# Last batch of a gated SSM + ternary FFN kernel worked tile by tile in halves of 512 columns, roundings on VectorE, a new order of all pieces

## The reference

```python
z = layernorm(x)
# selective state-space layer over ctx, 256 channels e, 16 states n, 256 steps l
u = silu(causal_conv4(in_proj @ ctx) + conv_b)
dt, Bm, Cm = split(x_proj @ u)                 # 8 + 16 + 16 rows
delta = softplus(dt_proj @ dt + dt_b)
state[e,n] = state[e,n] * exp(delta*A[e,n]) + delta*u*Bm[n]      # along l
y = (sum_n state*Cm[n] + D*u) * silu(z)
x = x + tanh(g_xattn) * y
# feed-forward with ternary weights and 8-bit tokens
h = layernorm(x)
q  = round(h * 128/absmax(h)) ; gate, up = q @ Wg, q @ Wu        # 256 -> 1024
i  = fwht(silu(gate) * up)                     # Walsh-Hadamard over 1024
q2 = round(i * 128/absmax(i)) ; x = x + tanh(g_ffn) * (q2 @ Wd)  # 1024 -> 256
```

## Time and profile before

| what | value |
|---|---|
| median of 3 runs | 239.27 us (238.29 to 240.78) |
| the profiled execution's own time | 238.49 us |
| its span, first to last instruction | 236.4 us |
| granted TensorE clock, mean | 0.909 |
| busy: DVE, PE, POOL, ACT | 78%, 75%, 71%, 70% |
| last store issued to the end | some 2 us |

### The profile page before, as it was taken

How to read it: one execution, slowest core, us unless ns; L and a number is a source line. 1 busy time by engine, 2 the same in 40 slices (tenths; PEclk the granted TensorE clock), 3 DMA queues, 4 the chain that set the end, 5 groups by cost and what they waited for, 6 DMA issues and landing times.

```text
span 236.4 us, 3708 instructions
## 1 busy us (share of the span) xinstructions
PE 177.0 (75%) x1216; PEld 144.1 (61%) x1216; DVE 185.4 (78%) x270; ACT 165.5 (70%) x285; POOL 168.6 (71%) x262
## 2 busy tenths in 40 slices
PE   3876859988987977788778599956746987575864
PEld 2545637977866966476677467745633776433752
DVE  3518986799999996999978946997668885579962
ACT  2499999996999983999956479968445614733230
POOL 1003079996799999999999999999999999500000
PEclk9985575599999999999979979999999999998895
DMA  3795000000000000000000000000000000000001
GB/s 65 224 348 217 1 1 0 4 0 0 3 0 3 0 0 4 0 0 1 3 1 0 0 0 3 22 25 1 0 0 3 24 22 3 0 22 0 3 22 44
DMA packets 8148, 6.33 MB, mean 27 GB/s; under 512 B 2202, under 2 KB 7874, under 8 KB 8130
## 3 DMA queue, kind: packets, MB, share of 16 engines
q1 hardware_dynamic: 7154, 6.02, 8.0%
q10 hardware_dynamic: 976, 0.09, 0.3%
HBM read 5.05 MB, written 1.05 MB: 26 GB/s over the span
## 4 chain that ended last, share of the span: by engine, by line
POOL 41%; ACT 21%; PE 15%; issue 9%; DVE 8%; DMA 3%; SPq 1%; POOLq 0%; DVEq 0%; ACTq 0%
POOL driveT L1276 11%; POOL wnat L1340 9%; POOL wnat L1341 9%; ACT decay L983 7%; POOL wq L1298 5%; DMA ctxs<-in_ctx_dram 3%; PE PY L468 2%; PE GP L598 2%; POOL q L1294 2%; DVE wnat L1604 2%; DVE wnat L1615 2%; ACT wq L1098 2%; DVE wnat L1614 1%; PE X L497 1%; PE BC L407 1%
## 5 line engine op out<-in xcount | busy, mean ns | idle before, releaser
L1276 POOL TENSOR_SCALAR driveT<-duT,BT 128x256 f32<-128x256 f32 x120 | 56.9, 500 | 13.7 <-ACT duT L1000 10.9
L983 ACT ACTIVATE decay<-delta,zero_c,aneg 128x255 f32<-128x255 f32 x128 | 64.9, 588 | 0.8 <-DVE state L1478 0.7
L1478 DVE TENSOR_TENSOR_SCAN state<-decay,BC 128x512 f32<-128x512 f32 x30 | 36.4, 1213 | 9.8 <-issue 6.9
L1478 DVE TENSOR_TENSOR_SCAN state<-decay,UP 128x512 f32<-128x512 f32 x30 | 36.1, 1203 | 5.7 <-issue 3.3
L1555 DVE TENSOR_TENSOR prod<-state,BC 128x1024 f32<-128x1024 f32 x32 | 38.3, 1198 | 1.1 <-DVE state L1478 0.8
L468 PE MATMUL PY<-id,prod 128*128 128x128 f32 x256 | 35.5, 284 | 1.4 <-DVE prod L1555 0.9
L468 PEld LDWEIGHTS PY<-id,prod 128*128 128x128 f32 x256 | 30.5, 147 | 3.0 <-DVE prod L1555 1.6
L1340 POOL TENSOR_TENSOR wnat<-wnat 128x512 f32<-128x512 f32 x18 | 22.9, 1274 | 0.9 <-DVE wnat L1604 0.2
L1341 POOL TENSOR_TENSOR wnat<-wnat 128x512 f32<-128x512 f32 x18 | 22.9, 1274 | 0.0
L1102 ACT COPY hT<-GP 128x1024 f32<-128x1024 f32 x8 | 8.1, 1008 | 21.2 <-PE GP L616 21.2
L407 PE MATMUL BC<-id,driveT 128*128 128x128 f32 x120 | 19.8, 291 | 3.2 <-POOL driveT L1276 2.2
(11 more groups left out here) (210 smaller groups left out, 390.5 us busy)
## 6 DMA issues: line engine op xcount, KB each, us to landing
wnat<-in_L_ffn_w_gate_dram SPq DMA_DIRECT2D x1, 1024.0 KB, 9.4
xs<-in_x_dram SPq DMA_DIRECT2D x1, 1024.0 KB, 11.8
wnat<-in_L_ffn_w_up_dram SPq DMA_DIRECT2D x1, 1024.0 KB, 11.9
wnat<-in_L_ffn_w_down_dram SPq DMA_DIRECT2D x1, 1024.0 KB, 11.3
out_dram<-ot SPq DMA_DIRECT2D x8, 128.0 KB, 1.7
ctxs<-in_ctx_dram SPq DMA_DIRECT2D x1, 384.0 KB, 6.9
ctxs<-in_ctx_dram SPq DMA_DIRECT2D x1, 128.0 KB, 2.7
inw<-n_L_xattn_in_proj_w_dram SPq DMA_DIRECT2D x1, 128.0 KB, 2.7
```

The lines of the kernel that those rows point to most:

```text
L983: last = nc.scalar.activation(decay[:, m % RING, h, n, 1:L], delta[:, b % 2, h, 1:L], ACT.Exp, bias=zero_c[:], scale=aneg[:, h, NB * j + n ...
L1276: last = nc.gpsimd.tensor_scalar(driveT[:, m % RING, c, n], duT[:, b % 2, c], BT[:, b % 2, c, NB * j + n:NB * j + n + 1], 1.0, ALU.mult, A ...
L1478: nc.vector.tensor_tensor_scan(state[:, g % STATES, h].rearrange("p n l -> p (n l)"), decay[:, g % RING, h].rearrange("p n l -> p (n l)"), ...
```

## The change

It has three parts.

1. **The roundings leave POOL.** `round_tokens_early` and `round_down_early` are gone. `round_tokens(f)` and `round_down(f, t)` on DVE do all of them. POOL's `second_rstd(3)` is gone too; DVE does it in `last_second_rstd`.
2. **The last batch in pieces.** Everything from the residual of batch 3 on has functions of its own, `last_...`, for one tile of 128 tokens, and from `last_gate` on for half of its 1024 columns, so one bank of PSUM. After the folds a half holds the even or the odd blocks of 128. The maximum of a tile is that of its halves, so `last_quant` waits for both. `q2_T` and `down` write into the banks that the Hadamard product used. Copies out of PSUM that DVE made for the last batches (`tokens_out`, `q2_out`) are ACT's now.
3. **A new order** of the pieces on PE, ACT, POOL and DVE from the first one on. Of these lists the diff below shows a few lines.

```diff
@@ POOL: gone @@
-            def round_tokens_early(f):
-                pool.wait_ge(act_xr, f + 1)
-                nc.gpsimd.tensor_scalar(q[:], xn[:], MAGIC + QB - 1, MAGIC, ALU.min, ALU.subtract).then_inc(rounded, 1)
-            def round_down_early(f, t):
-                pool.wait_ge(act_tq, LC * f + t + 1)
-                nc.gpsimd.tensor_scalar(q2[:, t], tq, MAGIC + QB - 1, MAGIC, ALU.min, ALU.subtract).then_inc(rounded_down, 1)
@@ ACT @@
+            def last_silu(t, i):
+                act.wait_ge(last_gated, 2 * t + i + 1)
+                act.wait_ge(last_gs, t + 1)
+                nc.scalar.activation(sg[:, t, 512 * i:512 * (i + 1)], last_half(ffn_bank(B - 1, t), i), ACT.Silu,
+                                     bias=zero_c[:], scale=gs[:, t:t + 1]).then_inc(last_sg, 1)
+            def last_quant(t, i):
+                act.wait_ge(last_sc, t + 1)
+                if t == 0:
+                    act.wait_ge(dve_q2, LC * (B - 1))
+                else:
+                    act.wait_ge(last_q2, i + 1)
+                nc.scalar.activation(tq[:, 512 * i:512 * (i + 1)], last_half(transform_bank(B - 1, t), i), ACT.Identity,
+                                     bias=magic_c[:], scale=sc2[:, t:t + 1]).then_inc(last_tq, 1)
...
@@ DVE @@
+            def last_second_rstd(c):
+                link = last_link[c]
+                dve.wait_ge(last_stat, c + 1)
+                dve.wait_ge(last_r, c + 1)
...
+            def last_absmax(t, i):
+                link = last_link[t]
+                dve.wait_ge(last_h, 2 * t + i + 1)
+                col = am3[:, t, i:i + 1]
+                link(nc.vector.tensor_reduce(col, last_half(transform_bank(B - 1, t), i), AX.X, ALU.max,
+                                             apply_absolute_value=True))
...
+            def last_round_down(t, i):
+                dve.wait_ge(last_tq, 2 * t + i + 1)
+                half = slice(512 * i, 512 * (i + 1))
+                nc.vector.tensor_scalar(q2[:, t, half], tq[:, half], MAGIC + QB - 1, MAGIC, ALU.min, ALU.subtract
+                                        ).then_inc(last_q2, 1)
@@ PE @@
+            def last_inter_T(t, i):
+                pe.wait_ge(last_folded, 4 * t + 3 + i)
+                if t == 1:
+                    pe.wait_ge(last_hT, i + 1)
+                for j in range(NI // 2):
+                    a = 2 * j + i
+                    last = nc.tensor.transpose(last_half(GP, i)[:, P * j:P * (j + 1)], fold[:, t, P * a:P * (a + 1)], id32[:])
+                last.then_inc(pe_last_tp, 1)
...
@@ order, ACT, start @@
-            for_silu()
             first_tap()
+            for_silu()
+            tanh_gates()
             xpw_out()
@@ order, POOL @@
             second_rstd(2)
-            round_down_early(1, 0)
+            drives(28)
             drives(29)
-            round_tokens_early(2)
+            drives(30)
             token_factors(2)
-            drives(30)
             drives(31)
-            round_down_early(1, 1)
```

More of the change, by code:

```diff
@@ new lines, in last_by, with last_gate @@
+            def last_by(t, i, w, done):
+                for h in range(HALF):
+                    last = nc.tensor.matmul(last_half(ffn_bank(B - 1, t), i), qT[:, h, P * t:P * (t + 1)],
+                                            w[:, h, 512 * i:512 * (i + 1)], start=(h == 0), stop=(h == HALF - 1))
+                last.then_inc(done, 1)
+            def last_gate(t, i):
+                pe.wait_ge(last_qT, t + 1)
+                if t == 0:
+                    pe.wait_ge(act_tp, LC * (B - 1))
+                else:
+                    pe.wait_ge(act_tq, LC * (B - 1) - 1)
+                last_by(t, i, wgT, last_gated)
@@ new lines, in last_hadamard @@
+            def last_hadamard(t, i):
+                pe.wait_ge(last_hT, 2 * t + i + 1)
+                if t == 0:
+                    pe.wait_ge(act_tq, LC * (B - 1))
+                else:
+                    pe.wait_ge(last_mul, 2 * LC)
+                for j in range(NI // 2):
+                    last = nc.tensor.matmul(last_half(transform_bank(B - 1, t), i)[:, P * j:P * (j + 1)],
+                                            hT[:, t, 2 * j + i, :], had[:], start=True, stop=True)
+                last.then_inc(last_h, 1)
@@ new lines, in last_q2_T, with last_down @@
+            def last_q2_T(t, i):
+                pe.wait_ge(last_q2, 2 * t + i + 1)
+                for j in range(NI // 2):
+                    last = nc.tensor.transpose(last_half(transform_bank(B - 1, t), i).bitcast(BF16)[:, P * j:P * (j + 1)],
+                                               q2[:, t, 512 * i + P * j:512 * i + P * (j + 1)], id16[:])
+                last.then_inc(pe_last_q2T, 1)
+            def last_down(t, i):
+                pe.wait_ge(last_q2T, 2 * t + i + 1)
+                for j in range(NI // 2):
+                    last = nc.tensor.matmul(transform_bank(B - 1, t)[:, 0:E], q2T[:, t, NI // 2 * i + j, :],
+                                            wdT[:, 2 * j + i, :], start=(i == j == 0), stop=(i == 1 and j == NI // 2 - 1))
+                if i == 1:
+                    last.then_inc(pe_dn, 1)
@@ L1238, in _ @@
             second_norm(2)
+            decays(30)
             for_silu()
@@ L1715, in _ @@
             times_C(6)
+            weight_out(1)
             scan(8, 0)
@@ L1780, in _ @@
             times_C(22)
-            result(0, 0)
             scan(24, 0)
@@ L1786, in _ @@
             scan(25, 0)
+            result(0, 1)
             scan(25, 1)
             times_C(24)
+            residual(2)
             scan(26, 0)
-            result(0, 1)
-            residual(2)
+            stats2(2, dve_ln_link)
+            absmax2(1, 0)
             scan(26, 1)
             times_C(25)
-            stats2(2, dve_ln_link)
-            absmax2(1, 0)
+            round_down(1, 0)
             scan(27, 0)
@@ L1798, in _ @@
             times_C(26)
-            scan(28, 0)
             token_scale(2, dve_ln_link)
             absmax2(1, 1)
+            round_tokens(2)
+            scan(28, 0)
             scan(28, 1)
+            round_down(1, 1)
             times_C(27)
+            result(1, 0)
             scan(29, 0)
```

652 lines of the change are left out of this document (381 added, 271 removed).

## The result

The changed kernel takes **224.08 us** (median of four runs, 223.40 to 224.99), against 239.17 us before (238.29 to 240.78): a ratio of 0.938, 95% interval 0.934 to 0.943. The forecast was 223.5 us. The profiled execution took 223.4 us, with a span of 221.6 us (before 236.4).

The account below looks back on a forecast made before the run. POOL was taken to bound the kernel from step 10 to the last sum in PY. Gains of 9.8 (roundings), 0 (start) and 5.3 us (last batch) took the profiled 238.49 us to 223.4, predicted as 223.5, range 218 to 231.

Parts of the forecast that it names:

- The sum of the middle: From step 10's `times_C` to the last sum in PY: DVE's 98.8 us plus 6 idle, 104.8 us, gain 9.8.
- The total: Whole kernel: gains of 9.8 + 0 + 5.3 = 15.1 us, giving 223.5 us.
- The idle time: DVE's in the middle: 2.1 us for the last sum, 2.6 walked, 1.3 for PE's queue, 6 us in all.
- The bound passes from POOL to DVE: In the middle, POOL's work falls from 112.3 to 91.9 us and DVE's rises to 98.8, so DVE binds.
- The chain's shares: In the chain of waits, POOL's share falls from 41% to under 15% and DVE's rises over 30%.
- The start: Up to step 10: one more open table load, 1.3 us, other moves offsetting; counted 0, 1.5 us either way.
- The last batch: From the last sum in PY to the last result: 32.6 us in four pieces against 37.9, gain 5.3 us.
- B: In the steps, DVE's idle time comes back as waits for ACT, 13 us idle; 230.5 us, chance 0.26.
- C: In the last batch, PE runs its small pieces at the low clock, 3 us more; 226.5 us, chance 0.09.
- D: Roundings in DVE's queue before scans wait for ACT at seven places, 19.2 us; 241.3 us, chance 0.05.
- E: POOL stays the bound because DVE locks it out, half of its 20.4 us kept; 228.5 us, chance 0.05.
- The table load's price: On ACT in the start: 1.28 us per load without the skill's 1.38 us drain, which would add 1.4 us.

Follow-up runs that it names:

- r_only: The kernel before with its own order and last batch, only the seven roundings moved from POOL to DVE; 230.26 us, ratio 0.960.
- t_only: The kernel before with only the new last batch; order up to the last step and POOL's roundings as before; 233.49 us, ratio 0.979.
- o_only: The changed kernel with its new order and last batch, but the seven roundings back on POOL; 248.01 us, ratio 1.038.
- pool_fill_after: The changed kernel with six extra additions of 512 columns on POOL, results unused; 230.80 us, ratio 0.964.
- dve_less: The changed kernel with four of DVE's absolute maxima over 1024 columns cut to 16 columns, output not the reference's; 224.74 us, ratio 0.937.

## Why the prediction was right, point by point

- **The sum of the middle** held: 104.8 us forecast, 104.62 in `r_only`, where nothing else is changed (gain 9.9 against 9.8), and 102.74 in the change, where 1.2 us of `weight_out` had moved ahead. DVE's sum was 98.8 against 98.74 in `r_only` (96.56 in the change), POOL's 92 to 96 against 94.5 and 93.4. That DVE's sum fits to 0.1 us is partly luck: in `r_only` the seven roundings took 5.4 us and not 4.05, and the rest of DVE's work took 93.3 us in place of 94.7.
- **The total** is partly luck too: the middle was 2.1 us shorter than forecast and the start 2.6 us longer, of which only the 1.2 us of `weight_out` are the same piece of work counted on the other side.
- **The idle time** held: 6 us forecast, 6.18 measured (102.74 less 96.56). The walk had 0.8 us at `token_scale(1)` and 1.0 at `round_tokens(2)`; the trace has 0.85 and 1.11, both for ACT, as named.
- **"The bound passes from POOL to DVE"** was wrong. Up to its last drive POOL is busy 97.5% and on the chain; the runs with more and with less work show that it still sets the pace there, with DVE right behind, and DVE only in the 18 us after it. The number came out, by luck as far as this step goes, since the two sums end close together: 82.55 us of POOL's work against 80.34 of DVE's. What should have warned me is that I compared sums over a stretch in which POOL's last drive must be done 15 us (in the change 18 us) before the end.
- **The chain's shares** were a bad test: POOL's was to fall under 15% and DVE's to rise over 30%; they are 25% and 11%.
- **The start** was counted at 0 within 1.5 us, with step 10 ending 1.3 us late and two more `weight_out` done. It ended 2.6 us late in the profile, with those two done. Of the table loads the prediction had the one of before right (from 3.16 us on, in ACT's wait), but it took only the second one of the change to be in the open. There the first one waits together with its activation, and both are in the open. Of the moves, ACT's wait for `x_dbl(1)` was 2.56 us (2.7 forecast); not foreseen was DVE's wait of 2.69 us at 41.35 for `C_rows(1)`, which stands behind `x_dbl(1)` on PE. Profiles at a like clock put the order's share at 1 to 3 us, with the two `weight_out` in it; closer than that it stays open, as the same code scatters by 3.1 us.
- **The last batch**, cut at the same events and counted from the start of the last sum (187.14; the 196.32 that the prediction calls its end is its start): 9.25, 4.11, 9.58 and 9.34 us, against 9.3, 4.3, 9.7 and 9.3. Sum 32.3 against 32.6, gain 5.6 against 5.3, and `t_only` shows it alone. Some 0.4 us of the 5.6 are not the new pieces but the clock: in `r_only`, which has the last batch of before, the last down product took 1.05 us in place of 1.89, and the end is 39.6 us in place of 40.1.
- **The rivals.** B (ACT) did not come: ACT ended waits of 0.85 and 1.11 us, no more (its sum, 223.4 + 7, is 230.4 and not 230.5). C (low clock): the clock was 0.99 in the end, against 0.89 before, so the shorter bursts did not lose it. PE's waits there, up to 1.2 us each, did not bring it to the 1.2 GHz level; only in the last 4.6 us was the mean below 1.00, at 0.92. The rule that I set beside it, from the Trainium skill ("TensorE: Matmul & The Clock Gate", Part 1), that the clock falls when TensorE has been little busy, is not contradicted by that, but the loss that I expected from it here did not come. D is what `o_only` looks like, but by POOL's roundings and PE's order. E named the right engine for the wrong reason and at the wrong price: of the 20.4 us taken off POOL only 2.6 came back in `r_only` (its sum fell from 112.31 to 94.54), where E had half of them come back.
- **The table load's price.** In the change, the instructions behind the loads start at 8.76 and 11.09, 0.02 and 0.01 us after the loads' ends at 8.74 and 11.08. The drain of 1.38 us that the Trainium skill counts ("ScalarE: Activation LUTs", What ACT_TABLE_LOAD costs) is not there; 1.28 us is the whole.

## What to carry to other kernels

Compare the engines' sums only over the stretch that ends where each engine's last needed piece ends; an engine can be "90% busy" over the whole and still have no gap where it matters. To find who binds, change the work of one engine at a time in both directions; more work cost something on either engine (7.5 of 7.6 us on POOL, 4.3 of 7.2 on DVE), while less work gave nearly nothing on DVE, and each time it helps to see which engine is then busy without a gap. When an operation moves to a faster engine and the order is changed with it, try each with the other left as it was: here the move brought its gain in the old order as well, and the new order without the move was 3.8% slower than the kernel before.

## What the runs showed that was not expected

DVE's rounding and POOL's work get in each other's way, in both directions. The same rounding of 512 columns took 0.43 us alone, but 1.39 us in `pool_fill_after`, where it began 0.16 us behind an addition of POOL:

```profile
86.61 1.39 DVE L1737 TENSOR_SCALAR q<-xn 128x512 bf16<-128x512 f32 x1
```

```profile
86.45 1.26 POOL L309 TENSOR_TENSOR delta<-spl,spr 128x512 f32<-128x512 f32 x1
```

It ended at 88.00, 0.29 us behind that addition's end (87.71), so it seems to have waited for that end with its first 0.14 us already behind it. Two roundings of `dve_less` that began inside a fold of POOL fit the same: they ended 0.55 and 0.54 us behind the fold's end, 0.13 to 0.14 us less than the 0.68 us that one takes alone. In `r_only` one took 1.78 us inside a row of drives of 0.48 us each; that is more than one drive's length, and what it waited for is open. In `dve_less`, roundings of 1024 columns that fell on POOL's folds or drives took 1.13, 0.81, 1.01 and 0.79 us in place of 0.70 on average, which gave back 0.9 of the 4.2 us saved. The other way round, POOL's pair of tiny pieces took 0.96 us beside a rounding and 0.52 otherwise. The Trainium skill ("SBUF — State Buffer", Who interferes with whom) says of a `tensor_scalar` on VectorE in a two-port mode that whoever issues first gets the shared pair of ports for the whole instruction, and the other one blocks. The 1.39 us agree with it; the 1.78 us, behind several drives, are longer than one such wait. It cost the change little: DVE's seven roundings took 4.3 us in its middle against 4.05 by their rows.
